# First mixing pass with its turns overlapped, bias added by the eviction, edge ends loaded in 112, 15 and 1 rows

## The reference

```
xn  = layernorm(x)                                  # no scale, no shift
# graph part: per node a row Wh = xn @ W.T + b and 4 + 4 attention scores from it
Wh  = xn @ W.T + b;  a_src, a_dst = scores of Wh    # 256 + 8 numbers a node
e   = leaky_relu(a_src[src] + a_dst[dst]);  att = softmax of e over the edges of one src
gnn = sum over edges of att * Wh[dst], by src
# mixing part: linear attention over all nodes
q, k, v = xn @ Wqkv.T;  k = elu(k) + 1
kv   = sum over ALL nodes of k (x) v;  ksum = sum over all nodes of k
t    = (q . kv) / (q . ksum + 1e-6), then layernorm, two dense layers, layernorm
x    = x + gnn + mix(xn)
out  = x + feed_forward(layernorm(x))               # shared and expert MLPs
```

## Time and profile before

| | |
|---|---|
| median of 3 runs | 3393.16 us (3389.64 to 3396.11) |
| profiled execution, its own time | 3393.59 us |
| its span | 3391.8 us |
| busy: PE, DVE, ACT, POOL | 67%, 56%, 23%, 64% |
| mean granted TensorE clock | 0.837 |
| first transfer of the scatter issued | 315.05 us |
| last one issued | 639.30 us |
| mixing pass, first instruction | 361.08 us |
| first instruction of stage two | 816.11 us |

### The profile page before, as it was taken

One profiled execution on the slowest core, in us unless ns is written; L12 is line 12 of the kernel. 1 busy time (PEld: TensorE's weight loads), 2 busy tenths in 40 slices (PEclk: granted clock), 3 DMA queues, 4 the chain that ended last, 5 costly groups with the idle time before them and its releaser, 6 DMA issues.

```text
span 3391.8 us, 41019 instructions
## 1 busy us (share of the span) xinstructions
PE 2288.1 (67%) x10919; PEld 1564.2 (46%) x10920; DVE 1906.6 (56%) x3902; ACT 773.7 (23%) x1397; POOL 2156.6 (64%) x2140
## 2 busy tenths in 40 slices
PE   0000466664477787877878787877877878787877
PEld 0000233332355555555555555555555555555555
DVE  5999321212455656556665656556664565646564
ACT  0000122221132222222222222222222222222222
POOL 0002777401676777777777777777777777777771
PEclk9555677877698988888899998989897988998888
DMA  2200011102333343444434443443434444343453
GB/s 64 108 0 1 26 44 32 38 28 52 103 94 106 100 122 101 109 115 102 122 102 123 103 122 102 109 117 102 123 101 106 120 102 122 102 122 102 111 108 38
DMA packets 271469, 305.58 MB, mean 90 GB/s; under 512 B 164198, under 2 KB 210796, under 8 KB 271020
## 3 DMA queue, kind: packets, MB, share of 16 engines
q0 software_dynamic: 97760, 251.60, 27.9%
q1 hardware_dynamic: 140038, 18.08, 3.4%
q10 hardware_dynamic: 33480, 33.36, 3.0%
HBM read 276.25 MB, written 26.62 MB: 89 GB/s over the span
## 4 chain that ended last, share of the span: by engine, by line
PE 39%; POOL 15%; DVE 11%; issue 9%; ACT 2%; DMA 1%; DVEq 0%; POOLq 0%; SPq 0%; ACTq 0%
PE sum_banks L937 20%; POOL gathered L863 15%; PE f_banks L952 8%; DVE onehot L1340 3%; PE turned L909 2%; PE f_banks L996 1%; DVE gathered L1361 1%; PE f_banks L1071 1%; DMA gathered<-table,col 1%; PE sum_banks L925 1%; PE f_banks L977 1%; PE f_banks L1072 1%; PE f_banks L978 1%; PE f_banks L966 1%; DVE he L1489 1%
## 5 line engine op out<-in xcount | busy, mean ns | idle before, releaser
L863 POOL DMA_INDIRECT gathered<-table,col x1872 | 1898.5, 1014 | 595.1 <-issue 564.5
L937 PE MATMUL sum_banks<-gathered,onehot 128*128 128x260 f32 x3744 | 1061.8, 446 | 104.9 <-DVE gathered L1361 104.0
L937 PEld LDWEIGHTS sum_banks<-gathered,onehot 128*128 128x128 f32 x3744 | 818.4, 224 | 294.9 <-issue 132.5
L1361 DVE TENSOR_TENSOR gathered<-gathered 128x512 f32<-128x512 f32 x936 | 591.4, 692 | 47.2 <-ACT gathered L1116 44.4
L1340 DVE TENSOR_TENSOR onehot<-iota_row,col 128x1024 f32<-128x1024 f32 x236 | 289.0, 1225 | 472.7 <-PE sum_banks L937 442.9
L270 POOL DMA_INDIRECT edge_list<-payload,pos x244 | 248.0, 1016 | 377.9 <-DVE pos L387 300.6
L1112 ACT COPY onehot_t<-turned 128x1024 bf16<-128x1024 bf16 x236 | 238.7, 1011 | 392.0 <-PE turned L909 391.4
L1126 ACT COPY acc<-sum_banks x234 | 88.0, 376 | 877.3 <-PE sum_banks L937 726.5
L909 PE MATMUL turned<-ident_bf,onehot 128*128 128x128 bf16 x1888 | 158.5, 232 | 190.2 <-DVE onehot L1340 189.8
L582 PE MATMUL bank<-ident,y 128*128 128x128 f32 x104 | 25.6, 427 | 278.0 <-DVE y L469 278.0
L909 PEld LDWEIGHTS turned<-ident_bf,onehot 128*128 128x128 bf16 x1888 | 116.1, 103 | 208.4 <-DVE onehot L1340 169.7
(11 more groups left out here) (304 smaller groups left out, 2722.6 us busy)
## 6 DMA issues: line engine op xcount, KB each, us to landing
gathered<-table,col POOLq DMA_INDIRECT x1872
table<-wh ACTq DMA_DIRECT2D x13, 520.0 KB, 3.1
xn<-y ACTq DMA_DIRECT2D x13, 512.0 KB, 2.9
xn_batch<-xn ACTq DMA_DIRECT2D x13, 512.0 KB, 4.0
x_all<-in_x SPq DMA_DIRECT2D x1, 6144.0 KB
x_batch<-in_x ACTq DMA_DIRECT2D x12, 512.0 KB
out<-xf ACTq DMA_DIRECT2D x12, 512.0 KB
edge_list<-xn_all SPq DMA_DIRECT2D x2, 2176.0 KB, 13.8
```

The lines of the kernel that those rows point to most:

```text
L863: g.indirect_dma_start(gathered[:, l, t, :], None, sh["table"], bass.IndirectOffsetOnAxis(ap=col[l][:, t // G, t % G, 0:1], axis=0)).then_ ...
L937: last = t.matmul(sum_banks[:, ds(banks_of[g], 1), 0:TB].rearrange("p a w -> p (a w)"), onehot[:, l % 3, g * G + k, :], gathered[:, l, g * ...
L1361: v.tensor_tensor(value, value, gathered[:, l, tiles, C:TB].unsqueeze(3).broadcast_to([P, G, H, HD]), ALU.mult).then_inc(s_mul, 1)
```

## The change

**Edge ends.** Rows 0 to 111, 112 to 126 and 127 come in three transfers instead of two, and the waits go to 48.

**Buffers.** y, xT and wh get a second buffer each, in memory that the sorting no longer uses (so these show as xn_all in a listing). s_kept and s_tab are one semaphore a buffer.

**Bias.** It is multiplied out once into 128 rows (b_all), and the eviction of the graph row becomes an addition on VectorE (table_rows) in place of ScalarE's copy. The matmul of the bias is gone from every block.

**Order.** A turn prepares the next: VectorE does mean and variance of turn it+1 behind block 0 and writes its y behind block 1; ScalarE takes the root at block 1, sends y behind block 2, and copies xT at the turn's end; TensorE transposes in front of the accumulation of block 3. The accumulation of block u-1 stands behind the products of block u. The loop holds two turns, one a buffer, with three turns written out ahead of it and two behind.

```diff
-                sp.dma_start(dst[0:P - 1, :], src[0:(P - 1) * TE].rearrange("(p t) -> p t", t=TE)).then_inc(s, 16)
+                for a, b in ((0, ROWS_EVEN), (ROWS_EVEN, P - 1)):
+                    sp.dma_start(dst[a:b, :], src[a * TE:b * TE].rearrange("(p t) -> p t", t=TE)).then_inc(s, 16)
-            dve.wait_ge(s_src, 32)
+            dve.wait_ge(s_src, 48)
...
+            def table_rows(it, q, uses, u):
+                dve.wait_ge(s_g, it * BATCH + u + 1)
+                if u == 0:
+                    wait_freed(dve, s_tab[q], uses * 16)
+                    wait_freed(dve, s_ad, max(it - 1, 0) if isinstance(it, int) else it - 1)
+                v.tensor_tensor(wh[q][:, u, :], banks[2 + u % 2][:, 0:C + 2 * H], b_all[:, :], ALU.add)\
+                    .then_inc(s_wh, 1)
...
+            def turn(it, q, uses, uses_next):                 # VectorE
+                done[0] = 0
+                dve.sem_clear(s_dve)
+                last_turn = isinstance(it, int) and it == ITERS - 1
+                table_rows(it, q, uses, 0)
+                keys_of(it, 0)
+                if not last_turn:
+                    moments(it + 1)
+                table_rows(it, q, uses, 1)
+                keys_of(it, 1)
+                if not last_turn:
+                    normalise(it + 1, 1 - q, uses_next, it)
+                table_rows(it, q, uses, 2)
+                keys_of(it, 2)
+                table_rows(it, q, uses, 3)
+                keys_of(it, 3)
...
+            def turn(it, q, uses, uses_next):                 # ScalarE
                 for u in range(BATCH):
                     n = it * BATCH + u
-                    s.copy(wh[:, u, :], banks[2 + u % 2][:, 0:C + 2 * H]).then_inc(s_wh, 1)
+                    if u == 1 and not last_turn:
+                        deviation(it + 1)
                     act.wait_ge(s_kmin, n + 1)
                     s.activation(k_exp[:, u % 2, :], k_min[:, u % 2, :], ACT.Exp).then_inc(s_kexp, 1)
                     act.wait_ge(s_nd, n + 1)
                     s.copy(vv[:, u % 2, :, 0:P], banks[4 + u % 2][:, C:2 * C].rearrange("p (a d) -> p a d", a=2))\
                         .then_inc(s_vc, 1)
+                    if u == 2 and not last_turn:
+                        keep(it + 1, 1 - q)
+                if not last_turn:
+                    turned_out(it + 1, 1 - q)
...
+            def turn(it, q, uses, uses_next):                 # TensorE
                 pe.wait_ge(s_xT, it + 1)
                 for u in range(BATCH):
                     wait_freed(pe, s_wh, it * BATCH + max(u - 1, 0))
...
-                    t.matmul(banks[2 + u % 2][:, 0:C + 2 * H], ones_row[:, :], b_row[:, :], start=False, stop=True)\
-                        .then_inc(s_g, 1)
...
-                    pe.wait_ge(s_kk, n + 1)
-                    pe.wait_ge(s_vc, n + 1)
+                    if u:
+                        accumulate(it, u - 1)
+                if not (isinstance(it, int) and it == ITERS - 1):
+                    transposes(it + 1, 1 - q)
+                accumulate(it, BATCH - 1)
```

More of the change, by code:

```diff
@@ L80, in wait_freed, with all_turns @@
         engine.wait_ge(semaphore, count)
[L83 to L87, removed]
+def all_turns(engine, turn):
+    for it in range(3):
+        turn(it, it % 2, it // 2, (it + 1) // 2)
+    with engine.Fori(0, (ITERS - 5) // 2) as j:
+        turn(j * 2 + 3, 1, j + 1, j + 2)
+        turn(j * 2 + 4, 0, j + 2, j + 2)
+    for it in range(ITERS - 2, ITERS):
+        turn(it, it % 2, it // 2, (it + 1) // 2)
 def stage_sort_and_mix(nc, A, sh):
@@ L448, in _, with moments @@
             dve.wait_ge(s_x, 32)
[L451 to L453 removed]
+            def moments(it):
                 for u in range(BATCH):
@@ L472, in one_turn @@
                 last.then_inc(s_xn, 1)
[L473 to L483, removed]
@@ L488, in _ @@
+            done[0] = 0
+            dve.sem_clear(s_dve)
+            moments(0)
+            normalise(0, 0, 0, 0)
+            dve.wait_ge(s_bias_out, 1)
+            all_turns(dve, turn)
             dve.wait_ge(s_acc, NBP)
@@ L543, in one_turn @@
                 act.dma_start(sh["table"][ds(it * W4, W4), :].rearrange("(b p) c -> p b c", p=P),
[L544 to L550 removed]
+                              wh[q][:, :, 0:TB]).then_inc(s_tab[q], 16)
+                s.copy(sh["ad"][:, ds(it * BATCH, BATCH), :], wh[q][:, :, C:C + H])
+                s.copy(sh["t8"][:, ds(it * BATCH, BATCH), 0:H], wh[q][:, :, C + H:C + 2 * H]).then_inc(s_ad, 1)
+            act.wait_ge(s_bias, 1)
+            s.copy(b_all[:, :], banks[5][:, 0:C + 2 * H]).then_inc(s_bias_out, 1)
+            deviation(0)
+            keep(0, 0)
+            turned_out(0, 0)
+            all_turns(act, turn)
+            for q in range(2):
+                act.wait_ge(s_kept[q], 16 * ((ITERS + 1 - q) // 2))
+                act.wait_ge(s_tab[q], 16 * ((ITERS + 1 - q) // 2))
         @block.tensor
@@ L576, in _, with transposes @@
             pe.wait_ge(s_gwc, 1)
+            t.matmul(banks[5][:, 0:C + 2 * H], ones_row[:, :], b_row[:, :], start=True, stop=True).then_inc(s_bias, 1)
+            pe.wait_ge(s_bias_out, 1)
             pe.wait_ge(s_kv0, 1)
-            def one_turn(it):
+            def transposes(it, q):
                 pe.wait_ge(s_xn, it + 1)
@@ L595, in one_turn @@
                     for k in range(2):
-                        last = t.matmul(banks[4 + u % 2][:, :], xT[:, k, P * u:P * u + P], w_kvg[:, k, 0:2 * C],
+                        last = t.matmul(banks[4 + u % 2][:, :], xT[q][:, k, P * u:P * u + P], w_kvg[:, k, 0:2 * C],
                                         start=k == 0, stop=k == 1)
                     last.then_inc(s_kv, 1)
-                    pe.wait_ge(s_kk, n + 1)
-                    pe.wait_ge(s_vc, n + 1)
-                    for a in range(2):
-                        last = t.matmul(banks[6][:, 129 * a:129 * a + 129], kk[:, u % 2, P * a:P * a + P],
-                                        vv[:, u % 2, a, 0:129], start=False, stop=False, skip_group_check=True)
-                    last.then_inc(s_acc, 1)
-            first_and_rest(pe, ITERS, one_turn)
+                    if u:
[3 more added lines that the diff above has]
+                accumulate(it, BATCH - 1)
+            transposes(0, 0)
+            all_turns(pe, turn)
 def stage_edges_and_feed_forward(nc, A, sh):
```

74 lines of the change are left out of this document (46 added, 28 removed).

## The result

| | before | after |
|---|---|---|
| median of 4 runs | 3394.64 us (3389.64 to 3400.24) | 3200.29 us (3195.71 to 3205.10) |
| profiled execution | 3393.59 us, span 3391.8 | 3205.10 us, span 3203.4 |
| pass: first statistics to the last copy to kv_bd | 361.1 to 815.8 | 335.2 to 549.0 |
| scatter: first and last issue | 315.05, 639.30 | 289.21, 612.28 |
| stage two starts | 816.11 | 616.58 |

The ratio of the runs is 0.9429, 95% interval 0.9411 to 0.9447: 194 us faster. In another job the same kernel had 0.9411 (0.9397 to 0.9426), 3191.33 us. The prediction was 3195.

A forecast was written before the change was run, and what follows sets the result against it. The pass was taken to bound stage one, with the scatter next. Stage two starting at 617.2 instead of 816.1 takes 198.9 us, 27.65 of it the load, off 3393.59: 3194.7, said as 3195, range 3185 to 3222.

The forecast's parts named there:

- The load, 27.65 us: Stage one's start: the 112-row load uses 16 engines, so line 301's counting starts at 10.6 instead of 38.25.
- The sign "10 to 11 us": Stage one's start: line 301 (now 314) would be seen to start at 10 to 11 us.
- The turn, 16.3 us: The pass at full clock: a turn takes 16.3 us, from blocks of 3.5, transposes of about 1.0 and small waits.
- The pass's end, 563: Stage one: first block at 346.4, 5 us for a slow first turn, then the remaining turns and kv_bd, ending at 563.
- The scatter, +2.4 us for five more turns beside it: GpSimd's scatter: 3.8 us laid on 8 turns, 0.48 each; five more turns beside it add 2.4, issues ending at 615.3.
- The signal of the last landing and the start of stage two: End of stage one: up to 1.6 us for the scatter's landing signal, then 0.3 until stage two starts.
- Stage two starts at 617.2: End of stage one: the scatter sets it, so stage two starts at 617.2 instead of 816.1, 54 us behind the pass.
- Stage two, 2576 us as before: Stage two: not touched by the change, so its 2576 us are carried over as they are.
- the 7 us that I had named: Stage two: the prediction would be wrong if its length changed by more than 7 us.
- Rival A: The pass: TensorE stays at half clock, turns take 30 us, the pass still sets stage one's end; 3310 us, chance 0.07.
- Rival B: The load: the 112 rows still crawl on one engine, gaining 0 to 3 us; time 3222, chance 0.07.
- rival C: Stage two: slower than before, TensorE's clock falling to 0.74 there, 250 us more; 3445 us, chance 0.02.

The follow-up runs named there:

- the kernel that beats both: Changed kernel with iota_row as GpSimd's first constant, counting waiting for it alone, and the places' look-up reading its shared operands from a bank: 3180.99 us, ratio 0.9368.
- sums at once: Changed kernel with each block's product added to the sums right behind that block's own products: 3191.02 us, ratio 0.9401; run again 3196.60 us, 0.9419.
- the bias as a matmul: Changed kernel with the bias again a one-row matmul in each block and ScalarE's copy evicting the graph row: 3198.59 us, ratio 0.9449.
- the kernel with own turns: Changed kernel with each turn making its own statistics, y and xT at its start, sums still one block late: 3212.42 us, ratio 0.9464.

## Why the prediction was right

It said 3195 by the scatter as the next bound, and the result is 3200.29 in the first job and 3191.33 in the second. The mechanism is the one named: the pass ends first, the engines wait 67 us for the scatter, and stage two starts when it has landed. That the start of stage two was met to 0.6 us is luck; three terms were off and cancelled. By its steps:

- **The load, 27.65 us.** 25.84 (12.41 for 38.25). The transfer came as said, at 297 GB/s. The step that was off is line 260's time, which I carried over as 10.57; it is 12.26. GpSimd's small operations now lie beside VectorE's first two operations on the edges, which used to come 28 us later, and two of them got longer: the memset of ones_sq takes 0.94 instead of 0.20, the selection behind it 0.97 instead of 0.29, together 1.4 of the 1.7 us. (In the kernel that beats both they lie there too and take 0.99 and 0.97.) VectorE's operations beside them have only one input. The prediction had asked what VectorE's additions do to the scatter, not what its first operations do to GpSimd's constants. With iota_row first the counting starts at 10.60; that it is the predicted 10.6 is chance, since there VectorE's own two operations are what ends last. The sign "10 to 11 us" failed. The Trainium skill (DMA: Bandwidth & Descriptors, "Why a DMA increments its semaphore by 16 and not by 1") gives 112 rows 16 engines; the busy share of 0.87 agrees.
- **The turn, 16.3 us.** 15.5 to 15.9, behind the first. A block without waits is 3.05 (409.63 to 412.68), not 3.5. I took 1.98, the length of the w_kvg row, as its slot, but the next matmul starts before that row is over: with the bias's row in the block the slots are 0.98, 0.64, 1.82 and 0.44 (454.91 to 458.79), without it 0.89, 1.71 and 0.45. VectorE's and ScalarE's chain comes out as worked out: the root at 3.7 behind the first block's products, as against 3.9, and y in time. The addition takes 0.43, as taken. The waits of 1.03 and 1.31 are over the 1 us that I had allowed.
- **The pass's end, 563.** 549.0, by the shorter blocks.
- **The scatter, +2.4 us for five more turns beside it.** Not there: from first issue to behind the last it is 324.3 us, 1.2 less than before. The 3.8 us that I had laid on eight turns are not of the turns: 3.3 of them are two pauses in the issuing, idle times of 2.18 us (at 473.38) and 1.69 us (at 616.53) where the others are 0.30. The changed kernel has two as well, and the second, 1.69 us ahead of the issue at 589.55, comes when the pass has long been over. The additions do not hold it: issues beside them are 0.96, the lower bound. Its last issue was predicted near 614 and came at 612.28.
- **The signal of the last landing and the start of stage two.** 3.0 us behind the last issue's slot (613.54 to 616.58); I had 1.9.
- **Stage two starts at 617.2.** 616.58. The load is 1.8 short, the scatter 3.6 better, the signal 1.1 longer: they cancel.
- **Stage two, 2576 us as before.** 2586.8 in the profile of the changed kernel, beyond the 7 us that I had named, so this sign of being wrong did show. It is the only sizeable difference between 3195 and that profile's 3205. Ten more profiles, with a stage two that no edit touched, took from 2568.5 to 2580.8, among them the same changed kernel with 2568.5. So the 11 us are not tied to the change. The traces show two differences that go with them. TensorE's longest wait, for VectorE's one-hot rows, is the same (151.5 and 152.0 us, from 184 us behind the start of the stage on), but its wait for scored is 10 us longer; before, and in the changed kernel:

```profile
PE scores L919 <- DVE scored L1349: 84.3, 51, 4.3
PE scores L989 <- DVE scored L1419: 94.4, 53, 6.3
```

VectorE's scored in turn waits for the gathered rows of the table: 79.8 us before, 86.0 in this profile, 51.9 in the one with 2568.5. And TensorE was at half clock for 641 us of the stage, 626 before. Neither alone orders the twelve profiles: stage two took 2572.3 us with 635 us at half clock (sums at once), and 2580.8 with 616 (the bias as a matmul), which has the longest wait for scored. No kernel was made for it, and why the gathered rows come later in one execution than in another is open.

Rival A (the pass as the bound, at the half clock) is refuted for this kernel, and the kernel with own turns shows that it was a real one: with one idle stretch of 3.1 to 3.7 us a turn the clock is 0.80 and the pass is the bound. The point from which it decides, 20.8 us a turn, is shown from both sides: at 20.4 the pass is hidden, at 21.3 stage two begins 7 us later. Rival B fell with the 297 GB/s; rival C, 200 to 250 us more in stage two, with a stage two that is 11 us longer at most.

Of the pass's shortening, 455 to 214 us, some 241, only 174 show. That is why the delayed sums (63 us of the pass) and the bias's move (27 us of it) can each be undone at no cost that the runs can tell.

## What to carry to other kernels

When two independent chains end in one meeting, price a speed-up of the longer only down to the shorter, and say from which length on it is worth nothing; here 67 us of a well made pipeline buy nothing, and two small edits on the other chain made stage one 14 us shorter. An engine that is not on the path can still hold one that is: look for an instruction that takes three times its median, and at what lay beside it. The length of a row is not its slot: take the time from one start to the next. A load moved earlier brings its consumers beside other work, so carry over no time from a stretch that used to be quiet.

## What the hardware showed

- One-row matmuls and the clock: with four more of them a block TensorE was 98% busy and was granted 0.84, the clock going to and fro between full and half; with four of 128 rows instead, equally busy, it was granted 1.00. One a block (17.5 us a turn) left it at 1.00.
- A gap of 1.76 us in three blocks of four left the clock at 1.00 through the whole pass; one of 3.1 to 3.7 us a turn, with one of 1.2 us behind the transposes, came with half clock in every turn (0.80 on the mean).
- VectorE holds GpSimd's indirect transfers at 2.72 to 3.58 us instead of 0.96 when both its inputs lie outside the banks. When one is in a bank they take 0.96, at the same length of its own operation (3.33 and 3.34). The Trainium skill (SBUF — State Buffer, "Who interferes with whom") says the first of this, that two inputs in SBUF make such an instruction contend with a GpSimd one that reads SBUF; the runs agree, for transfers whose places lie in SBUF. For two inputs the page names the shared read side, where the prediction speaks of the pair.
- Beside operations of VectorE with one input (128x1612, 1.0 to 1.1 us) a memset and a selection of GpSimd over 128x128 took 0.94 and 0.97 us instead of 0.20 and 0.29.
- ScalarE went from the root to the exponential in 1.3 us (413.67 to 414.97), all of it table load.
